# A recommendation model on one core: the last part of the batch by feature groups, layer 0 without transposes back

## The reference

```python
def _bn(x, g, b):
    return g * (x - x.mean(0)) * rsqrt(x.var(0) + EPS) + b
x = dense_inputs
for W, b, g, be in bot:                      # 13 -> 512 -> 256 -> 64
    x = _bn(relu(x @ W + b), g, be)
T = concatenate([embs, x[:, None, :]], 1)    # [B, 27, 64]
Z = einsum('bnd,bmd->bnm', T, T)
R = concatenate([x, Z[:, iu, ju]], 1)        # pairs above the diagonal
h = R
for W, b, g, be in top:                      # 415 -> 512 -> 256 -> 1
    h = _bn(relu(h @ W + b), g, be)
return sigmoid(h)
```

## Time and profile before

| | us |
|---|---|
| timed runs, median of 3 | 589.19 (588.45 to 590.12) |
| span of the profiled execution | 987.2 |
| first gather starts / last gather starts (profiled) | 4.50 / 857.19 |
| first transpose of part 15 (profiled) | 920.02 |
| first matmul of top layer 1 (profiled) | 950.20 |
| TensorE busy | 448.2 (45%) |
| VectorE busy | 233.0 (24%) |
| ScalarE busy | 189.5 (19%) |
| GpSimd busy | 401.1 (41%) |

### The profile page before, as it was taken

The page is one execution under the profiler, slowest core; times in us unless marked ns, Lnnn a source line. Parts: engine busy times, 40 slices in busy tenths (PEclk is TensorE's granted clock), DMA queues, the critical chain, the costliest instruction groups (busy, mean ns, idle before and its releaser), DMA issues.

```text
span 987.2 us, 13898 instructions
## 1 busy us (share of the span) xinstructions
PE 448.2 (45%) x5827; PEld 321.1 (33%) x5827; DVE 233.0 (24%) x640; ACT 189.5 (19%) x509; POOL 401.1 (41%) x426
## 2 busy tenths in 40 slices
PE   7751151624425161523517162351715244177787
PEld 3430020513214051412405051240514133165664
DVE  6600130402112040312204031220403022055542
ACT  5400020302011030302103030210303021044523
POOL 6777227072542707163361706336171634500000
PEclk9975575756657575755757575575757557577999
DMA  5122001020110202010110101011020101100000
GB/s 168 23 27 26 12 9 26 3 26 10 18 18 11 26 3 27 7 23 14 14 23 5 26 6 23 14 14 23 5 27 6 24 13 15 22 3 1 3 1 0
DMA packets 15895, 18.30 MB, mean 19 GB/s; under 512 B 7614, under 2 KB 8894, under 8 KB 15695
## 3 DMA queue, kind: packets, MB, share of 16 engines
q0 software_dynamic: 13312, 13.66, 10.6%
q1 hardware_dynamic: 2524, 3.72, 1.2%
HBM read 17.34 MB, written 0.01 MB: 18 GB/s over the span
## 4 chain that ended last, share of the span: by engine, by line
another core or an unknown queue 61%; PE 23%; ACT 10%; issue 3%; DVE 3%; DMA 0%; ACTq 0%; SPq 0%; DVEq 0%
PE l_bank L469 11%; ACT Zs L280 7%; PE l_bank L409 3%; PE l_bank L393 2%; PE l_bank L466 2%; PE l_bank L399 1%; PE l_bank L423 1%; ACT TT L636 1%; PE z_bank L455 1%; PE l_bank L507 1%; PE tr_bank L351 1%; DVE TT L853 1%; ACT hidden L582 0%; ACT hidden_hi L648 0%
## 5 line engine op out<-in xcount | busy, mean ns | idle before, releaser
L320 POOL DMA_INDIRECT emb<-table,stage x390 | 374.3, 960 | 424.1 <-DVE stage L802 309.2
L455 PE MATMUL z_bank<-TT 64*27 64x26 f32 x3840 | 127.5, 217 | 403.5 <-issue 388.4
L455 PEld LDWEIGHTS z_bank<-TT 64*27 64x27 f32 x3840 | 89.2, 132 | 442.9 <-issue 442.9
L254 DVE COPY Zs<-z_bank 27x112 f32<-27x112 f32 (+3 forms) x272 | 88.2, 324 | 498.7 <-remote 488.6
L280 ACT ACTIVATE Zs<-z_bank 27x112 f32<-27x112 f32 (+3 forms) x272 | 91.6, 337 | 552.8 <-remote 535.2
L469 PE MATMUL l_bank<-Zs,tw_sb 128*128 128x128 f32 x840 | 117.1, 298 | 0.0
L469 PEld LDWEIGHTS l_bank<-Zs,tw_sb 128*128 128x128 f32 x840 | 112.6, 215 | 0.0
L853 DVE COPY TT<-tr_bank 128x512 f32<-128x512 f32 (+1 forms) x60 | 51.1, 979 | 4.2 <-PE tr_bank L441 3.9
L351 PE MATMUL tr_bank<-idle_operand 128*128 128x512 bf16 x112 | 46.9, 590 | 0.0
L864 DVE BATCH_NORM_STATS2 stats_t<-h_block 128x128 f32 x60 | 17.7, 294 | 123.8 <-ACT hidden_hi L648 123.8
L441 PE MATMUL tr_bank<-ident,emb 128*128 128x128 f32 x195 | 30.8, 284 | 35.1 <-DVE TT L853 28.8
(11 more groups left out here) (120 smaller groups left out, 282.5 us busy)
## 6 DMA issues: line engine op xcount, KB each, us to landing
emb<-table,stage POOLq DMA_INDIRECT x416
tw_sb<-tw0x SPq DMA_DIRECT2D x1, 1792.0 KB
bw_sb<-bw SPq DMA_DIRECT2D x1, 512.0 KB
tw_sb<-tw SPq DMA_DIRECT2D x1, 512.0 KB
twx_sb<-twx SPq DMA_DIRECT2D x1, 256.0 KB
idx_raw<-idx SPq DMA_DIRECT2D x1, 169.0 KB, 3.0
bw_sb<-bw SPq DMA_DIRECT2D x2, 64.0 KB
hidden<-dense_t SPq DMA_DIRECT2D x1, 104.0 KB
```

The costliest lines, as they stand in the source:

```text
L254: last = copy(dst, src[:, :, ZC * q:ZC * q + w])
L320: pool.indirect_dma_start(out=emb[:, s, k, h, :], out_offset=None, in_=table, in_offset=bass.IndirectOffsetOnAxis(ap=stage[:, s, col:col + ...
L455: mm = nc.tensor.matmul(bank[QUAD * j:QUAD * j + V, x * ZM:(x + 1) * ZM], one, one[:, 1:V], start=True, stop=True)
```

## The change

- The last part's half 1 has four groups of table pairs, 0 to 3, 4 to 7, 8 to 11 and 12. Half 0 keeps its three.
- x moves from the last column of `TT` to the first, in the loop too. A column m of Z is now stored in tile c = m' // 4 and quarter q = m' mod 4 of `Zs`, so that a group of 8 embeddings fills two whole tiles. The copies read every fourth column of a Z bank. The weights are laid out to match.
- For half 1 the Z matmuls are issued group by group: all vectors so far against the 8 (or 2) new columns. `take_last` copies a group's columns to `Zs`, and layer 0 is accumulated tile by tile as they come.
- Layer 0 of the last part has outputs as rows and all 128 samples as columns, as in the loop, so `pre0`, the transposes back and the half ReLUs go. Its tiles are multiplied for both halves at once, behind the copies of half 1.
- VectorE aggregates the statistics of parts 0 to 14 behind half 0's copies, and joins them with the last part's in a short aggregate of 9 numbers a block (`merged`).
- ScalarE makes the high parts of the last part (`last_hi`) behind the scaling of the weights; TensorE waits for the low parts only before the last 512 columns of layer 1.
- Samples stand in natural order, so that the sigmoid writes plain rows. `TT` for half 1 is cleared at the start. The fillers on TensorE are set anew.

```diff
-LAST_GROUPS = ((0, 8), (8, 12), (12, 13))
+LAST_GROUPS = (((0, 8), (8, 12), (12, 13)), ((0, 4), (4, 8), (8, 12), (12, 13)))
...
+def quadrant_columns(q, c0=0, c1=ZC):
+    return range(q + NQ * c0, min(q + NQ * c1, NF), NQ)
+def group_tiles(k0, k1):
+    return k0 // 2, (k1 + 1) // 2
...
+        def take_last(copy, g, quadrants):
+            c0, c1 = group_tiles(*LAST_GROUPS[1][g])
+            m0, m1 = NQ * c0, min(NQ * c1, NF)
+            rows = m1 + 1
+            for j in quadrants:
+                src = last_z_bank[1][g][QUAD * j:QUAD * j + rows, 0:RX * (m1 - m0)].rearrange(
+                    "p (x m) -> p x m", m=m1 - m0)
+                for q in range(NQ):
+                    m = quadrant_columns(q, c0, c1)
...
+                    last = copy(dst, src[:, :, m[0] - m0:m[-1] + 1 - m0:NQ])
...
-                if net == "top":
-                    pe.wait_ge(last_lo, K0)
                 for ch in range(CHUNKS):
+                    if net == "top" and ch == CHUNKS - 1:
+                        pe.wait_ge(last_lo, K0)
...
+            last_z(last_z_bank[0], 0, 0, NF)
+            pe.wait_ge(l0_relu, LAST * K0)
+            last_layer0(-1)
             last_transposes(1, 0)
             keep_clock(2, tr_bank[1])
-            pe.wait_ge(l0_relu, LAST * K0)
-            last_layer0_with_back(0)
+            last_z_group(0)
+            last_taken(1)
             last_transposes(1, 1)
+            last_taken(2)
+            last_layer0(0)
+            last_layer0(1)
+            last_z_group(1)
+            keep_clock(2, tr_bank[0])
+            last_taken(3)
+            last_layer0(2)
             last_transposes(1, 2)
-            last_back(0, 1, pre0_v, last_relu_v)
-            keep_clock(1, z_bank[0])
-            last_z(1)
-            keep_clock(5, tr_bank[1])
-            last_layer0_with_back(1)
-            last_back(1, 1, pre0_v, last_relu_v)
+            last_layer0(3)
+            last_transposes(1, 3)
+            last_z_group(2)
+            last_z_group(3)
+            last_taken(4)
+            last_layer0(4)
+            last_layer0(5)
+            last_taken(5)
+            last_layer0(6, (0, 2, 1, 3))
...
-            nc.scalar.activation(prob[:, :, :].rearrange("p b u -> p u b"),
-                                 logits[:, :].rearrange("p (u b) -> p u b", u=CU), ACT.Sigmoid,
+            nc.scalar.activation(prob[:, :], logits[:, :], ACT.Sigmoid,
...
             nc.vector.memset(Zs[:, :, :], 0.0).then_inc(cleared, 1)
+            nc.vector.memset(TT[0:D, 1, :, :], 0.0).then_inc(cleared, 1)
...
+            take_z(nc.vector.tensor_copy, last_z_bank[0], 0, (0, 1)).then_inc(last_taken_v, 1)
+            dve.wait_ge(top0_stats, LAST * K0)
+            nc.vector.memset(merged[:, :, 0:1], float(LAST * 2 * UNIT))
+            for o in range(K0):
+                last = nc.vector.bn_aggr(merged[:, o, 1:3],
+                                         stats["top", 0][:, o, :, :].rearrange("p a b -> p (a b)"))
+            last.then_inc(earlier_stats, 1)
+            dve.wait_ge(earlier_stats, 1)
+            nc.vector.tensor_scalar_mul(merged[:, :, 2:3], merged[:, :, 2:3],
+                                        float(LAST * 2 * UNIT)).then_inc(earlier_stats, 1)
+            last_lower(1, 0)
             last_take(0)
...
+            for n, o in enumerate((0, 2, 1, 3)):
+                dve.wait_ge(last_relu, n + 1)
+                nc.vector.bn_stats(merged[:, o, 3:9], h0_part[:, o, :]).then_inc(top0_stats, 1)
```

More of the change, by code:

```diff
@@ L70 @@
 CHUNKS = B // CHUNK
-CU = CHUNK // UNIT
 PW = NF
@@ L529, in _, with last_z, last_z_group @@
-            for g in range(len(LAST_GROUPS)):
+            def last_z(bank, h, m0, m1):
+                for x in range(RX):
+                    for j in range(NQ):
+                        one = TT[0:D, h, x * NQ + j, :]
+                        mm = nc.tensor.matmul(bank[QUAD * j:QUAD * j + m1 + 1, x * (m1 - m0):(x + 1) * (m1 - m0)],
+                                              one[:, 0:m1 + 1], one[:, m0 + 1:m1 + 1], start=True, stop=True)
+                mm.then_inc(last_z_done, 1)
+            def last_z_group(g):
+                first = len(LAST_GROUPS[0])
+                pe.wait_ge(last_tt_v, first + g + 1)
+                if g < len(LAST_GROUPS[1]) - 1:
+                    pe.wait_ge(last_tt_a, first - 1 + g + 1)
+                c0, c1 = group_tiles(*LAST_GROUPS[1][g])
+                last_z(last_z_bank[1][g], 1, NQ * c0, min(NQ * c1, NF))
@@ new lines, in last_layer0 @@
+            def last_layer0(c, blocks=range(K0)):
+                part = slice(LAST * 2 * UNIT, B)
+                for o in blocks:
+                    cols = slice(o * P, (o + 1) * P)
+                    if c < 0:
+                        mm = nc.tensor.matmul(l0_bank[o][:, 0:2 * UNIT], twx_sb[:, cols], x_all[:, part],
+                                              start=True, stop=False)
+                    else:
+                        mm = nc.tensor.matmul(l0_bank[o][:, 0:2 * UNIT], tw0_sb[:, c, cols], Zs[:, c, :],
+                                              start=False, stop=(c == ZC - 1))
+                    if c == ZC - 1:
+                        mm.then_inc(last_l0, 1)
@@ L600, in layer1 @@
                                          scale=norm[net, 0][:, 8, k:k + 1]).then_inc(scaled_a[net, 0], 1)
+                if net == "top":
+                    for o in (0, 2, 1, 3):
+                        nc.scalar.activation(hidden0["hi"][:, o, LAST * 2 * UNIT:B], h0_part[:, o, :],
+                                             ACT.Copy).then_inc(last_hi, 1)
                 act.wait_ge(bias_ready[net, 0], 1)
@@ L679, in _, with last_take @@
[L679 to L682 removed]
+            def last_take(g):
+                act.wait_ge(last_z_done, 2 + g)
+                take_last(act_copy, g, (2, 3)).then_inc(last_taken_a, 1)
+            last_upper(0, 0)
+            last_upper(0, 1)
@@ L977 @@
     for row, (n, m) in enumerate(zip(*np.triu_indices(V, k=1))):
-        q, c = divmod(m - 1, ZC)
-        tw0x[QUAD * q + n, c] = w0[D + row]
+        first, second = (0, n) if m == NF else (n + 1, m)
+        c, q = divmod(second, NQ)
+        tw0x[QUAD * q + first, c] = w0[D + row]
     arrays = {
```

211 lines of the change are left out of this document (76 added, 135 removed).

## The result

| | before | after |
|---|---|---|
| timed, median (range) | 589.06 (588.45 to 590.12) | 594.75 (593.46 to 595.2) |
| ratio, 95% interval | | 1.0099 [1.008, 1.0119] |
| profiled execution: its time, its span | 588.54, 586.7 | 594.39, 592.6 |
| last gather starts; lands (T) 2.6 later | 529.46; 532.1 | 528.18; 530.8 |
| first matmul of top layer 1 | 549.78 = T + 17.7 | 556.11 = T + 25.3 |

The change makes the kernel 1.0% slower, 5.7 us. I had forecast 588.8, with 592.8 as the upper end: wrong. The timed medians are of four runs each. The profile in the middle column is a second one of the kernel before, which was taken with the experiments; it isn't stretched as the one of the earlier trace rows was, and nor is the one after, so that the two columns can be compared line by line. Their spans differ by 5.9, close to the timed 5.7.

The account below looks back on a forecast made before the run. GpSimd's gathers were taken to bound the kernel, with a serial engine chain in the tail eating the gain: 589.19 + 0.2 (layer 1 at T + 17.1 against T + 16.9) - 0.6 (sigmoid) = 588.8 us, range 584.5 to 592.8.

Parts of the forecast that it names:

- What bounds the kernel: Whole kernel: GpSimd's 416 gathers set T = 531.5; before, the tail is paced by landing and layer 1 starts at T + 16.9.
- s: Moment when TensorE turns to the last part, with its first transpose; taken as T - 15.3.
- half 0 ends at T - 2.5: Last part, before: half 0 needs 12.8 us, ends at T - 2.5, and half 1 then waits for its gathers.
- aggregates 2.5: VectorE, between half 0's copies and half 1's first: four long aggregates 2.1, with memset and product 2.5 us.
- strided reads 0: Copies reading every fourth float of a Z bank: taken as 0, upper bound +2.6 us.
- sigmoid -0.6: Output: natural order lets the sigmoid write plain rows, -0.6 us on the path; bounds 0 and -0.6.
- The low parts on GpSimd: Four of 0.45 us, due only before layer 1's last quarter; worth 0, beside VectorE's weight scaling bound 0 to +1.
- Z group: Each group of half 1: 64 matmuls of 8 columns take 0.9 to 1.3 us, taken 1.1, plus 0.2 until copies start.
- tiles 0 and 1 at 1.2 GHz, +1.8: Layer 0 after TensorE's wait for VectorE's aggregates: half clock costs +1.8 us, plus 0.4 for Z and filler beside.
- Rival B: Slower: clock stays at half past tile 3, tiles 2 to 6 and fillers cost more; +3, 592 us; chance 0.25.
- C: The change does what it says, gathers pace the tail: layer 1 at T + 9.5, 7 us less, 581.5; chance 0.05.
- A: Faster: after keeps 2.4 GHz, before ran half 1's layer 0 at half clock; about 586.0 us; chance 0.33.

## Why the prediction was wrong

- *What bounds the kernel:* right in the main. Gathers set T, and s was forecast at T - 15.3 and is T - 15.2 (515.61). The tail of before was forecast at T + 16.9 and is T + 17.7. That half 0 ends at T - 2.5 and the tail is paced by the landing alone was wrong: the stretched profile had all gathers landed, and so hid the 3.90 us for which transposes wait in front of ready work. Half 0 ends at T + 1.9 and T + 0.5 in the two traces with before's order.
- *The chain from s, early part:* aggregates 2.5 (measured 2.0 of work), copies 1.8 (1.77 and 1.86), final aggregate 0.5 (0.40), strided reads 0 (112 elements: 2.79 for 8 copies, 2.81 before), sigmoid -0.6 (-0.5): right. The low parts on GpSimd: w_lo took 2.08 instead of 1.67 with GpSimd beside it, and layer 1's bias was in time, so 0 as written. The first set's copies were due at s + 13.9 and ended at s + 15.3, because half 0's copies began at s + 5.8 and not s + 4.8 and the first set's 2.1 behind its start and not 1.3, less 0.5 of shorter aggregates. The prediction's "per half" is a slip: only half 1 has more sets.
- *The step that failed:* "Z group: 64 matmuls again ... between 0.9 and 1.3, I take 1.1, plus 0.2." The third set took 3.8 from its start (540.36) to its copies (544.12), the fourth 3.5 more (547.62), where 1.3 and at most 1.8 stood in the sum: 4.5 us of gaps, part of which lies beside copies: from the third set's start to tile 4 it is 7.1 where 3.1 stood. I had priced execution alone. The row that says otherwise was shown: 2.03 of "issue" between 133 and 123 records in the earlier trace rows, and 368 waits of that kind in the earlier trace rows, which I called a fault of the profile. Their number was one, not their kind or length: the second trace of before has 15 such waits in the loop, 18.8 us in all, the longest 1.9, where the earlier trace rows has 368, 388.4 and 2.6.
- *The clock:* tiles 0 and 1 at 1.2 GHz, +1.8: right (3.75 for 16 records, 2.0 over the forecast 1.8). Rival B, half clock past tile 3, came true for tiles 4 to 6: 5.49 instead of 2.7, +2.8. I had its cause wrong (whether the run of tiles brings the clock back; it did, 1.00 in 539 to 543): it was lost again behind the gaps. So it was in six of the seven traces that have gaps of over 1.5 us in the tail; with two sets it held. The 15 fillers were not at half: 3.19 for 14.
- *Sum:* 32.4 forecast from s, + 1.7 up to the third set's start (s + 24.8 instead of 23.1), + 4.0 from there to tile 4 (7.1 instead of 3.1, the gaps less what lies beside copies), + 2.4 from tile 4 to layer 1 (8.6 instead of 6.2, the half clock) = 40.5 measured. The first term was wrong by a little in many places, the second is the step that failed, the third followed it.
- *Rivals of the prediction:* C, gathers pace it, didn't apply; A had the wrong sign, and layer 0 of half 1 at half clock, on which it built, is seen in one of two traces of before's program, with layer 1 at T + 18.0 and not T + 19.4.

That the gaps are TensorE's supply of instructions is shown as far as this goes: they follow the count of instructions, not of columns (before at full width, after at 2 to 10 columns), and stand at the same places in the stream, 256 apart, whatever the order of work; one 16.4 KB packet of the instruction queue stands 2.3 to 2.9 us ahead of each end of a gap; and they go when sets go. The Trainium skill, page "Runtime: NRT & Kernel Launch", section "Instruction fetch mechanics", says that an engine's instructions come in 16 KiB blocks of 256. The trace agrees: 256 instructions between two gaps, and the packet's size. The Trainium skill calls the crossing from block to block mostly hidden there; here it was not: 256 such instructions execute in 1.24 us, and the next ones were there after 3.45. What inside the chip makes a block take that long is open, and so is what decides when a packet is sent.

## What to carry to other kernels

Splitting a stream of tiny matmuls to start earlier multiplies the instructions, not the work: look for "issue" gaps at equal counts of records before you price a set by its busy time, and where nothing long stands between, price 256 TensorE instructions at what they took here from gap to gap, 3.45 to 3.8 us (four cases). A clock held with fillers is worth something only if instructions are there to use it; otherwise the gap comes sooner, and the fillers are instructions themselves. Two sets whose second one stands early in the queue were the best of the kernels tried, 583.58 us.
